# Folding the setup stage of a decoder-block kernel into its first real stage

## What is computed

```python
xn = _layernorm(x, ln_gamma, ln_beta)
k = einsum('btc,dc->btd', xn, Wk); v = einsum(.., Wv); r = einsum(.., Wr)
td = sigmoid(time_decay); tf = sigmoid(time_first)
kv = k * v
csum = cumsum(kv * power(td, t_idx), axis=1)
wkv = tf * kv + td * shifted(csum)
out = einsum('btc,dc->btd', sigmoid(r) * wkv, Wo)
x = _layernorm(x + out)
...
group_scores  = l2norm(x) @ l2norm(group_centroids).T      # in the expert part
expert_scores = l2norm(x) @ l2norm(expert_centroids).T + bias
```

## Time and profile before

| | us |
|---|---|
| median of 3 runs | 2131.97 |
| lowest, highest run | 2131.47, 2137.92 |
| profiled execution, its time | 2134.5 |
| profiled execution, its span | 2132.7 |

### The profile page before, as it was taken

One profiled execution on the slowest core, in us unless ns is written; L12 is line 12 of the kernel. 1 busy time (PEld: TensorE's weight loads), 2 busy tenths in 40 slices (PEclk: granted clock), 3 DMA queues, 4 the chain that ended last, 5 costly groups with the idle time before them and its releaser, 6 DMA issues. The chain is left out here.

```text
span 2132.7 us, 51909 instructions
## 1 busy us (share of the span) xinstructions
PE 1984.1 (93%) x14320; PEld 1787.2 (84%) x14320; DVE 1530.2 (72%) x3648; ACT 1254.4 (59%) x3478; POOL 1478.0 (69%) x1691
## 2 busy tenths in 40 slices
PE   5999879999999999785999999999999999489997
PEld 5777668888887888675999999999999999468886
DVE  5888747777787788763777778888888888335554
ACT  3555446666666666532777777777777777224443
POOL 3656512777677677663677778888888888459764
PEclk9999999999999999997999999999999999789999
DMA  3300022432422423304666766777777777367542
GB/s 122 109 0 0 0 94 80 139 101 79 158 79 90 147 79 118 110 21 139 228 230 228 232 228 227 236 237 237 237 235 229 230 233 234 110 242 241 182 168 99
DMA packets 244904, 329.89 MB, mean 155 GB/s; under 512 B 50074, under 2 KB 167234, under 8 KB 244836
## 3 DMA queue, kind: packets, MB, share of 16 engines
q1 hardware_dynamic: 218788, 279.97, 40.5%
q0 software_dynamic: 26048, 49.10, 6.3%
HBM read 236.17 MB, written 77.18 MB: 147 GB/s over the span
## 5 line engine op out<-in xcount | busy, mean ns | idle before, releaser
L1336 POOL DMA_INDIRECT slot_token<-a_entry,a_slot_i x256 | 261.4, 1021 | 113.2 <-issue 71.8
L1818 POOL DMA_INDIRECT part_rows<-e_out,e_dest x184 | 211.0, 1147 | 74.2 <-issue 65.9
L1951 ACT ACTIVATE e_sg<-e_g 128x256 f32<-128x256 f32 x368 | 141.8, 385 | 204.7 <-PE e_g L1643 204.7
L1810 POOL DMA_INDIRECT e_xg<-x_rows,e_tok x188 | 196.5, 1045 | 85.1 <-issue 56.3
L2000 DVE TENSOR_TENSOR e_h<-e_sg,e_u 128x256 f32<-128x256 f32 x368 | 158.0, 429 | 100.4 <-PE e_u L1643 40.5
L1161 ACT ACTIVATE a_prob<-a_s,a_ntop 128x128 f32<-128x128 f32 x512 | 180.8, 398 | 3.0 <-DVE a_ntop L1515 2.9
L1826 POOL TENSOR_TENSOR e_wd1l<-e_raw_d,e_wd1h 128x256 fp32r<-128x256 f32 x184 | 145.5, 825 | 19.1 <-ACT e_wd1h L1931 18.4
L1826 POOL TENSOR_TENSOR e_wd0l<-e_raw_d,e_wd0h 128x256 fp32r<-128x256 f32 x184 | 145.9, 827 | 14.4 <-ACT e_wd0h L1931 13.6
L2015 DVE TENSOR_SCALAR e_out<-e_d,e_dest 128x256 f32<-128x256 f32 x184 | 80.6, 480 | 103.1 <-PE e_d L1643 103.1
L1643 PE MATMUL e_d<-e_wd1h,e_ht1h 128*128 128x256 f32 x368 | 109.4, 297 | 24.6 <-issue 24.6
L1023 PE MATMUL a_o<-a_wo,a_ot 128*128 128x256 f32 x512 | 123.1, 384 | 8.2 <-DVE a_ot L1582 8.2
(11 more groups left out here) (398 smaller groups left out, 7603.2 us busy)
## 6 DMA issues: line engine op xcount, KB each, us to landing
e_raw_g<-in_eg SPq DMA_DIRECT2D x94, 512.0 KB
e_raw_u<-in_eu SPq DMA_DIRECT2D x94, 512.0 KB, 5.6
e_raw_d<-in_ed SPq DMA_DIRECT2D x93, 512.0 KB
part_rows<-a_zero SPq DMA_DIRECT2D x16, 2048.0 KB
f_part<-part_rows SPq DMA_DIRECT2D x16, 2048.0 KB, 9.5
x<-in_x SPq DMA_DIRECT2D x16, 512.0 KB, 3.7
x_rows<-x SPq DMA_DIRECT2D x16, 512.0 KB
out_rows<-f_res SPq DMA_DIRECT2D x16, 512.0 KB, 10.2
```

The costliest lines, as they stand in the source:

```text
L1336: pool.indirect_dma_start(k.slot_tok, bass.IndirectOffsetOnAxis(ap=slot_i[:, j, q:q + 1], axis=0), entry[:, j, q, :], None, bounds_check=S ...
L1810: pool.indirect_dma_start(xg[a][:, n, :], None, k.x2_d, bass.IndirectOffsetOnAxis(ap=tok[a][:, n, 0:1], axis=0))\
L1818: pool.indirect_dma_start(k.part_d, bass.IndirectOffsetOnAxis(ap=dest[a][:, n, 1:2], axis=0), out[a][:, n, :], None).then_inc(put[a], 16)
L1951: act.activation(sg[m % 2][:], bank_g[m % 2][:, 0:SETW], ACT.Silu).then_inc(sg_rdy, 1)
```

## The change

The setup stage is gone as a block of its own; its work is placed inside the mixer's prologue.

- SP issues group 0 of x first, then the weights k, v, r, then the four small vectors, then the weight o, the centroids and the two biases. The biases now count on `cen_in`.
- POOL fills the constants first, takes `root` of group 0, then waits for the sum of the centroids' squares and takes their root, then `root` of group 1.
- ACT waits for the four vectors, takes the two sigmoids, scales the weights, and only then norms group 0.
- DVE: moments 0, low weights, moments 1, squares of the centroids, remainders of group 0, offsets, decay tables, normalised centroids. The copy of `cent` stands in period 0 between the first sum and the second half's product.
- PE computes the offsets of k and v, transposes group 0, and then computes those of r. The centroids are transposed in period 0, between the first projections and the transposes of group 1, into a bank that is not in use yet.
- The centroids and their squares live in `y[1]`, which is first written in period 1.

```diff
-                setup_stage(nc, k, dram)
                 mixer_stage(nc, k, dram)
@@ sync
                 sp.dma_start(grouped(rows(k.x, 0)), dram["x"].rearrange("b t d -> t b d")[:, 0:TG, :]).then_inc(x_in, 16)
-                for n in "kvro":
+                for n in "kvr":
                     sp.dma_start(w[n][:], dram["w" + n].rearrange("(c p) n -> p c n", p=P)).then_inc(w_in, 16)
+                with nc.allow_non_contiguous_dma(reason="short vectors"):
+                    for dst, src in ((k.gam, dram["gam"]), (k.bet, dram["bet"]), (td, dram["td"]), (tf, dram["tf"])):
+                        sp.dma_start(dst[:], src.rearrange("(c p) -> p c", p=P)).then_inc(vec_in, 16)
+                sp.dma_start(w["o"][:], dram["wo"].rearrange("(c p) n -> p c n", p=P)).then_inc(w_in, 16)
+                sp.dma_start(cen[0:G], dram["gcen"]).then_inc(cen_in, 16)
+                sp.dma_start(cen[G:G + E], dram["ecen"]).then_inc(cen_in, 16)
...
@@ tensor
+                    if isinstance(g, int) and g == 0:
+                        pe.wait_ge(cent, 4)
+                        for c in range(DC):
+                            last = pe.transpose(bank_o[1][:, c * (G + E):(c + 1) * (G + E)], cen[:, c * P:(c + 1) * P],
+                                                k.ident[0:G + E, 0:G + E])
+                        last.then_inc(cen_t, 1)
...
-                offsets()
+                pe.wait_ge(w_in, DMA + 64)
+                pe.wait_ge(vec_in, 64)
+                offsets("kv")
                 turn(0)
-                pe.wait_ge(low_rdy, ONE + LOWS)
+                offsets("r")
+                pe.wait_ge(low_rdy, ONE + 3 * DC)
@@ scalar
+                act.wait_ge(vec_in, 64)
+                act.activation(k.td[:], td[:], ACT.Sigmoid).then_inc(sig, 1)
+                act.activation(k.tf[:], tf[:], ACT.Sigmoid).then_inc(sig, 1)
+                weights_high()
                 norm_in(0)
-                weights_high()
                 turned(0, 0)
@@ gpsimd
                 root(0, 0, TG)
+                pool.wait_ge(cent, 1)
+                pool.tensor_tensor(nrm[:, 1:2], nrm[:, 0:1], half[0:G + E, :], ALU.pow).then_inc(fill, 1)
                 root(1, 0, TG)
+                pool.wait_ge(table, TABLES)
@@ vector
                 moments_in(0)
+                weights_low()
                 moments_in(1)
-                weights_low()
+                centroid_squares()
                 turned_low(0, 0)
+                offsets_kept()
+                decays()
+                centroids_normed()
                 dve.wait_ge(low_rdy, ONE + LOWS)
```

More of the change, by code:

```diff
@@ L90, in sem @@
         return self.ctx.enter_context(self.nc.semaphore(self.tag + name))
[L93 to L162, removed]
-                dve.wait_ge(cen_in, 32)
-                dve.tensor_tensor(sq[:], cen[:], cen[:], ALU.mult).then_inc(table, 1)
-                dve.wait_ge(table, 5 + 3 * DC)
-                dve.tensor_reduce(nrm[:, 0:1], sq[:], AX.X, ALU.add).then_inc(cent, 1)
-                dve.wait_ge(fill, 10)
-                dve.tensor_scalar(nrm[:, 2:3], nrm[:, 1:2], 1e-12, None, ALU.max).then_inc(cent, 1)
-                dve.wait_ge(cent, 2)
-                dve.reciprocal(nrm[:, 3:4], nrm[:, 2:3]).then_inc(cent, 1)
-                dve.wait_ge(cent, 3)
-                dve.tensor_scalar(cen[:], cen[:], nrm[:, 3:4], None, ALU.mult).then_inc(cent, 1)
-                dve.wait_ge(cen_t, 1)
-                dve.tensor_copy(k.cent[:], tp[:, 0:DC * (G + E)].rearrange("p (c e) -> p c e", c=DC)).then_inc(cent, 1)
-            @block.tensor
[L177 to L183, removed]
@@ L211, in mixer_stage @@
         p = Parts(nc, ctx, "m_")
+        td, tf = p.sb("td", [P, DC]), p.sb("tf", [P, DC])
+        zero = p.sb("zero", [P, T])
+        nrm, half = p.sb("nrm", [G + E, 4]), p.sb("half", [P, 1])
+        vec_in, cen_in = p.sem("vec_in"), p.sem("cen_in")
+        fill, sig = p.sem("fill"), p.sem("sig")
+        table, cent, cen_t = p.sem("table"), p.sem("cent"), p.sem("cen_t")
+        FILLS, TABLES = 10, 4 + 3 * DC
         w = {n: p.sb("w" + n, [P, DC, D]) for n in "kvro"}
@@ L632, in period, with decays, centroid_squares, centroids_normed @@
                     summed(g, 1)
+                def decays():
+                    dve.wait_ge(sig, 2)
+                    dve.wait_ge(fill, FILLS)
+                    dve.wait_ge(table, 4)
+                    for c in range(DC):
+                        dve.tensor_scalar(k.decay[:, c, :], k.ones[:], k.td[:, c:c + 1], None, ALU.mult).then_inc(table, 1)
+                        dve.wait_ge(table, 5 + 3 * c)
+                        dve.tensor_tensor_scan(k.decay[:, c, :], k.decay[:, c, :], zero[:], 1.0, ALU.mult, ALU.add)\
+                           .then_inc(table, 1)
+                        dve.wait_ge(table, 6 + 3 * c)
+                        dve.memset(k.decay[:, c, T - 1:T], 0.0).then_inc(table, 1)
+                def centroid_squares():
+                    dve.wait_ge(cen_in, 64)
+                    dve.tensor_tensor(sq, cen, cen, ALU.mult).then_inc(table, 1)
+                    dve.wait_ge(table, 4)
+                    dve.tensor_reduce(nrm[:, 0:1], sq, AX.X, ALU.add).then_inc(cent, 1)
+                def centroids_normed():
+                    dve.wait_ge(fill, FILLS + 1)
+                    dve.tensor_scalar(nrm[:, 2:3], nrm[:, 1:2], 1e-12, None, ALU.max).then_inc(cent, 1)
+                    dve.wait_ge(cent, 2)
+                    dve.reciprocal(nrm[:, 3:4], nrm[:, 2:3]).then_inc(cent, 1)
+                    dve.wait_ge(cent, 3)
+                    dve.tensor_scalar(cen, cen, nrm[:, 3:4], None, ALU.mult).then_inc(cent, 1)
+                def centroids_kept():
+                    dve.wait_ge(cen_t, 1)
+                    dve.tensor_copy(k.cent[:], bank_o[1][:, 0:DC * (G + E)].rearrange("p (c e) -> p c e", c=DC))\
+                       .then_inc(cent, 1)
+                dve.memset(zero[:], 0.0).then_inc(table, 1)
+                dve.memset(k.count[:], 0.0).then_inc(table, 1)
+                dve.memset(k.wkv_in[:], 0.0).then_inc(table, 1)
                 for n in "kv":
```

30 lines of the change are left out of this document (27 added, 3 removed).

## The result

| | us |
|---|---|
| kernel before, median of 6 runs | 2133.51 (2131.47 to 2137.92) |
| changed kernel, median of 6 runs | 2122.14 (2119.23 to 2125.78) |
| ratio | 0.9945, 95% interval 0.9932 to 0.9958 |
| span of the profiled execution, before and changed | 2132.7, 2122.1 |

The changed kernel is 11.4 us faster by the medians, 10.6 by the two traces. 2121.5 was predicted, a gain of 10.5. The median before now stands on six runs and lies 1.5 us above that of the first three; taken from it, the same gain would give 2123.0.

What follows compares the result with a forecast made beforehand. PE was taken to pace the kernel from the first projection on. That projection at 9.04 + 8.35 = 17.4 us instead of 28.28 gives 10.9, less 0.4 in period 0: 2131.97 - 10.5 = 2121.5 us, range 2115.5 to 2130.5.

Steps and rivals of the forecast that it cites:

- request for x: Start of the kernel: x is asked for at 0.9 us, between 0.79 and 1.20, instead of 12.79.
- vectors in the queue: Four small vectors ahead of the weight o delay the last weight by 1.2 us, bounds 0.5 to 2.8.
- last weight: Prologue: the last weight is there at 0.9 + 6.94 + 1.2 = 9.04 us, bounds 8.2 and 10.9.
- last weight to transposes: Prologue: ACT's scalings and norms take 4.54 us, and PE's transposes start about 0.3 us after ACT.
- first projection: PE in the prologue: starts at 9.04 + 8.35 = 17.4 us instead of 28.28, 10.9 earlier.
- added up to group 1: Period 0: two transposes of centroids between PE's products add 0.4 us.
- signs named beforehand: Marks expected in the trace, among them group pitch near 14.0 us and every later stage entry 10 to 11 us earlier.
- chain of waits: Whole kernel: waits followed back from the last instruction are PE work, so a head start should arrive whole at the end.
- dear vectors: Rival, request queue: vectors cost 2.8 us and the request comes at 1.20, total 2123.4; chance 0.10 together with late table.
- late table: Rival, ACT: table load of 1.28 us behind the vectors' wait, 0.9 us more, 2124.3; chance 0.10 together with dear vectors.
- DVE held ahead of the remainders: Rival, prologue: DVE waits for group 1 of x and the biases; 1.4 us lost, 2122.9, or 2124.9; chance 0.06.
- pitch of the loop: Rival, mixer loop: another phase adds 1.0 us a group, 14 us over 14 groups, total 2135.5; chance 0.04.
- used-up head start: Rival, downstream stages: dearer stage entries take 5 us or so, total 2127; chance 0.08 together with no such effect.

Runs made afterwards that it cites:

- late: The changed kernel with the small tensors requested first and waited for, and only then x and the weights; median 2128.96 us.
- again: The changed kernel run once more without any edit, for a second trace; median 2123.8 us, ratio 0.9953 to the kernel before.
- lean: The changed kernel with SP's requests reordered, separate semaphores for k and v, r, and the rest, and sigmoids behind group 0's norm; median 2122.53 us.
- lean_table: The lean kernel with one throwaway sigmoid of constants as ACT's first activation, ahead of its waits; median 2121.78 us.
- old_order: The changed kernel with the old order on ACT (norm of group 0, then weights) and PE (all offsets, then transposes); median 2123.16 us.
- vec_act: The changed kernel with the four small vectors issued from ACT instead of SP; median 2125.87 us.
- apart: The vec_act kernel in which, besides, ACT and PE wait for k and v only, then for r, each with its own semaphore; median 2125.03 us.

## Why the prediction was right

Step by step, predicted and measured:

| step | predicted | measured |
|---|---|---|
| request for x | 0.9 | 0.92 |
| vectors in the queue | 1.2 (0.5 to 2.8) | 7.82 - 6.94 = 0.88 |
| last weight | 9.04 | 8.74 |
| last weight to transposes | 4.84 | 4.50 |
| transposes to first projection | 3.5 | 3.42 |
| first projection | 17.4 | 16.66 |
| added up to group 1 | 0.4 | 0.76 |
| loop and end of the mixer | 0 | -0.8 |
| later stages | 0 | 1.0 |
| whole | -10.5 | -10.6 by the traces, -11.4 by the medians |

The mechanism held up to group 1. The first projection came 11.62 us earlier: x was asked for 11.87 earlier, the vectors took 0.88 of that back, and the way from the last weight to the first projection was 7.92 us instead of 8.55. The last weight set the pace, behind it ACT's scaling and norming (8.72 to about 13.2) as one uninterrupted piece, then transposes, copies, remainders. Offsets of r and remainders ended 0.15 us apart, as reckoned. Everything that was said to be hidden was: sigmoids, squares, decays, norming of the centroids, the root on POOL.

Two terms were too large. The vectors cost 0.88 us, not 1.2; of my bounds the lower, their busy time, was nearer. (One trace isn't sharp here: in the five kernels with these requests, the last weight came 7.25 to 7.91 us after the request for x, and without vectors in the queue 6.94 or, in late, 7.19, which makes the vectors 0.1 to 1.0.) And I gave ACT to PE a hop of 0.3 us where 13.24 - 13.19 = 0.05 was measured. One was too small: period 0 lost 0.76 instead of 0.4, though the transposes with the gap around them cost only 0.34. Most of the rest is the moment from which PE's products run closer: 4.34 us after the first product here, 19.78 - 16.77 = 3.01 in again, 3.49 in the kernel before. This I had put into the range, and again gave 0.6 us of it back: from the first projection to group 1 it took 11.87 us, here 12.49. The 0.8 us that the loop returned and the 1.0 that the later stages took weren't in the sum; that they nearly cancel was luck.

Two of the signs named beforehand didn't come as named. The later stage entries were 11.65, 8.5 and 10.2 us earlier, not 10 to 11, and the shift of 11.36 at 95 us was 10.6 at the end. With runs of one kernel several us apart, one pair of traces can't tell this from scatter. And the chain of waits that I had taken as a sign of PE's pace is followed back over only 7% of the span, all of it in the last stage; that the head start travels is borne by late instead.

Of the rivals, dear vectors fell by their landing time. A late table didn't occur: the sigmoids stayed ACT's first activation, and the load ran at 1.19; lean shows what it costs when a scaling comes first, 1.28 us on the path. DVE held ahead of the remainders was close: DVE came free at 14.72, and both remainders of 0.69 us would still have been in time from 15.2, so the cover was 0.5 us, not 0.9; group 1 of x had landed at 12.24 and not at 11.4. The variant that moved ACT forward (lean_table) and the one that moved DVE back (old_order) both ran into exactly this. The pitch of the loop did change, but by 1.0 us over 14 groups and downwards, not by 14 upwards. A used-up head start can be judged by late only against the changed kernel, where none was used up; against the kernel before, the medians gained 11.4 and 10.9 us of a shift of 11.65 and 12.2 at the attention entry, so 0.3 to 1.3 us may have gone, less than the medians scatter by.

## What to carry to other kernels

A setup stage costs its latency, not its work. Asking for the data earlier gave 0.3 us while the setup's chain, now behind the bulk in the queue, and a barrier stood between; the overlap with x asked for at 7.76 gave 5.4, both together 11.6. When work is moved ahead of the first useful product, look at each in-order engine for what now waits in front of the item on the path: a load of the next tile, a table that a new first activation asks for, a norm that isn't due. Small element-wise loads can stay in the same queue as the bulk, behind what is needed first: in the two kernels that asked for them early through a second queue they landed no sooner.

## What the runs showed of the hardware

- Four vectors of 256 single elements in a full queue delayed the transfer behind them by 0.88 us in the changed kernel, 0.2 us each (0.1 to 1.0 over five kernels, against two without the vectors). From a second queue, issued 1.8 us earlier, the last of them landed 0.2 us later (vec_act) and 1.0 later (apart), and the weight r needed 5.7 and 6.0 us instead of 4.6 to 5.4.
- ACT's table load stood at 1.19, ahead of the wait, with a sigmoid first. With a scaling first it stood at 7.79, behind its waits, and the later sigmoids loaded another. Why the one went ahead of a wait and the other did not, the runs don't show. After the load of 1.28 us the next activation followed within 0.02 us.
- Gamma, beta, k and v were there at 7.76, 6.99 and 7.92 in three kernels with equal requests: a landing time from one trace is good to about 1 us.
- PE's 512-column products ran closer together, 0.23 us from one start to the next instead of 0.43, from some moment after the first projection on: 3.0 us in again, 23.42 - 17.31 = 6.1 in apart. The granted clock reads 1.00 before and after it in both the changed kernel and apart, and no run shows what sets the moment. From the first product to group 1 it was 11.87 us in again, 12.49 in the changed kernel and 13.33 in apart, with the same work.
